# Which PSUM bank holds each head's exponents, and where the first four heads stand in TensorE's order

## The reference

```
x = x + gat(LN(x), adj)      # scores, softmax over allowed edges, probabilities @ wh
x = x + mamba2(LN(x))        # 8 heads, one chunk of 256 tokens
x = x + relational(LN(x))    # four relations, masks (adj == r) times x, times weight[r]
x = x + moe(LN(x))           # 8 experts, one per token, ReLU between two products
```

```
Lmat = exp(segsum(dA))
Y_diag = einsum('bcln,bcsn,bhcls,bcshp->bclhp', Cc, Bc, Lmat, xdt)
```

## Time and profile before

| | us |
|---|---|
| median of 3 runs | 3670.32 (3669.29 to 3671.39) |
| the profiled execution | 3668.25 |
| its span | 3666.5 |
| TensorE busy | 3470.5 (95%) |
| VectorE busy | 2562.8 (70%) |
| GpSimd busy | 1808.5 (49%) |
| ScalarE busy | 1776.8 (48%) |

### The profile page before, as it was taken

How to read it: one execution, slowest core, us unless ns; L and a number is a source line. 1 busy time by engine, 2 the same in 40 slices (tenths; PEclk the granted TensorE clock), 3 DMA queues, 4 the chain that set the end, 5 groups by cost and what they waited for, 6 DMA issues and landing times.

```text
span 3666.5 us, 64685 instructions
## 1 busy us (share of the span) xinstructions
PE 3470.5 (95%) x20028; PEld 2838.1 (77%) x20028; DVE 2562.8 (70%) x7429; ACT 1776.8 (48%) x3627; POOL 1808.5 (49%) x2010
## 2 busy tenths in 40 slices
PE   7999999999999999999999999999699999999998
PEld 5777777777777777777777777777488888888887
DVE  5878888887888888788888878888444444444444
ACT  4556655655655555565565556555232323323232
POOL 3545554454554545545454554545354555545453
PEclk8999999999999999999999999999799999999999
DMA  3121111111111111111111111111155555556563
GB/s 104 39 46 36 35 40 43 37 42 41 37 38 40 40 37 46 37 37 40 37 42 35 46 37 37 40 38 33 58 199 194 196 190 193 193 192 197 194 196 128
DMA packets 166001, 301.92 MB, mean 82 GB/s; under 512 B 37376, under 2 KB 138240, under 8 KB 147776
## 3 DMA queue, kind: packets, MB, share of 16 engines
q0 software_dynamic: 38272, 196.40, 15.7%
q1 hardware_dynamic: 91536, 70.58, 6.3%
q10 hardware_dynamic: 36144, 34.35, 6.0%
HBM read 248.61 MB, written 52.65 MB: 82 GB/s over the span
## 4 chain that ended last, share of the span: by engine, by line
PE 51%; DVE 26%; POOL 12%; issue 8%; ACT 1%; DVEq 0%; DMA 0%; ACTq 0%; POOLq 0%; SPq 0%
PE bank L1337 13%; PE bank L1351 13%; PE bank L1083 7%; POOL masks L466 7%; DVE conv L798 6%; PE bank L1101 5%; PE bank L1189 4%; DVE y L966 3%; PE bank L1289 3%; DVE y L971 2%; POOL row L452 2%; POOL rstd L452 2%; DVE stats L779 2%; DVE xn L789 1%; PE bank L1220 1%
## 5 line engine op out<-in xcount | busy, mean ns | idle before, releaser
L732 ACT ACTIVATE decay<-bank,w_up 128x256 f32<-128x256 f32 x568 | 269.4, 474 | 700.3 <-PE bank L1337 694.5
L1083 PE MATMUL bank<-xn1T,w_in 128*128 128x256 f32 x2304 | 523.4, 381 | 15.3 <-issue 14.3
L1337 PE MATMUL bank<-zs,w_up 128*128 128x256 f32 x2272 | 504.6, 380 | 0.6 <-ACT zs L590 0.6
L1351 PE MATMUL bank<-w_dn,decay 128*128 128x256 f32 x2272 | 502.1, 379 | 0.0
L1101 PE MATMUL bank<-w_rel,hT 128*128 128x256 f32 x2048 | 492.7, 384 | 0.0
L1083 PEld LDWEIGHTS bank<-xn1T,w_in 128*128 128x128 f32 x2304 | 434.1, 190 | 72.3 <-issue 14.0
L798 DVE SCALAR_TENSOR_TENSOR conv<-bank,conv_w,conv 128x255 f32<-128x255 f32 (+2 forms) x960 | 461.3, 481 | 34.8
L1337 PEld LDWEIGHTS bank<-zs,w_up 128*128 128x128 f32 x2272 | 433.4, 191 | 60.3 <-issue 0.9
L1351 PEld LDWEIGHTS bank<-w_dn,decay 128*128 128x128 f32 x2272 | 426.2, 190 | 55.1
L1044 DVE TENSOR_TENSOR hT<-bank,w_dn 128x256 f32<-128x256 f32 x142 | 60.3, 424 | 537.1 <-PE bank L1351 537.1
L1101 PEld LDWEIGHTS bank<-w_rel,hT 128*128 128x128 f32 x2048 | 368.9, 190 | 62.8 <-ACT hT L590 13.0
(11 more groups left out here) (219 smaller groups left out, 6341.4 us busy)
## 6 DMA issues: line engine op xcount, KB each, us to landing
token_rows<-row SPq DMA_DIRECT2D x64, 258.0 KB, 2.7
xT_sb<-in_xT ACTq DMA_DIRECT2D x64, 256.0 KB
x_sb<-in_x ACTq DMA_DIRECT2D x64, 256.0 KB, 2.7
adj_sb<-in_adj SPq DMA_DIRECT2D x64, 256.0 KB, 3.0
adjt_sb<-in_adjT SPq DMA_DIRECT2D x64, 256.0 KB, 3.0
out<-row SPq DMA_DIRECT2D x64, 256.0 KB, 2.2
w_in<-token_rows,idc POOLq DMA_INDIRECT x142
out<-hT,ids POOLq DMA_INDIRECT x142
```

The source lines that it names most:

```text
L732: nc.scalar.activation(hid(f), bank[f % 4][:, 0:GROUP], ACT.Relu, bias=b1[q % 2][:, f:f + 1]).then_inc(hid_ready, 1)
L1083: ins = mm(dst, w_in[:, k, first:first + P], xn1T[:, k, :], start=k == 0, stop=k == DK - 1)
L1337: ins = mm(bank[f % 4][:, 0:GROUP], w1[i][:, k, f * P:(f + 1) * P], xgT[:, k, :], start=k == 0, stop=k == DK - 1)
L1351: ins = mm(bank[4 + j][:, 0:D], hid(f)[:, j * P:(j + 1) * P], w2[i][:, f, :], start=f == 0, stop=f == FB - 1)
```

## The change

Each head gets a bank of its own choice, `EXPO = (2, 5, 1, 3, 4, 2, 5, 3)`. Head 2 uses bank 1, head 3 bank 3 and head 4 bank 4; heads 5, 6 and 7 take banks 2, 5 and 3 after the exponentials of heads 0, 1 and 3. Head 2 waits for `wh_ready`, head 3 for the first `xdt`, head 4 for the second. On TensorE `expo(range(0, 4))` moves in front of the turned probabilities. On ScalarE the exponentials of heads 0 and 1 move in front of the copy `probT`. The product of line 1249 waits in addition for the exponential of head 2.

```diff
-    EXPO = (2, 5, 3, 4)
+    EXPO = (2, 5, 1, 3, 4, 2, 5, 3)
 ...
                     ins.then_inc(prob_ready, 1)
-                    act.wait_ge(prob_turned, b1_ + 1)
-                    need(act, hp_made, b1_)
-                    copy(probT[:], bank[0][:, :]).then_inc(probT_ready, 1)
-                if b2_ is not None:
-                    for h in range(H):
+                for h in range(H):
+                    if h == 2 and b1_ is not None:
+                        act.wait_ge(prob_turned, b1_ + 1)
+                        need(act, hp_made, b1_)
+                        copy(probT[:], bank[0][:, :]).then_inc(probT_ready, 1)
+                    if b2_ is not None:
                         act.wait_ge(expo_made, 8 * b2_ + h + 1)
 ...
-                        nc.scalar.activation(decay[:, h, :], bank[EXPO[h % 4]][:, 0:TRI], ACT.Exp).then_inc(decay_ready, 1)
+                        nc.scalar.activation(decay[:, h, :], bank[EXPO[h]][:, 0:TRI], ACT.Exp).then_inc(decay_ready, 1)
 ...
-            def expo(heads, b):
+            def expo(heads, b, b1_):
 ...
-                    elif h in (2, 3):
-                        pe.wait_ge(xdt_ready, 2 * b + h - 1)
+                    elif h == 2:
+                        if b1_ is not None:
+                            pe.wait_ge(wh_ready, b1_ + 1)
+                    elif h in (3, 4):
+                        pe.wait_ge(xdt_ready, 2 * b + h - 2)
                     else:
-                        pe.wait_ge(decay_ready, 8 * b + h - 3)
+                        pe.wait_ge(decay_ready, 8 * b + {5: 1, 6: 2, 7: 4}[h])
 ...
                 if b3_ is not None:
                     relate(1, range(0, 2))
+                if b2_ is not None:
+                    expo(range(0, 4), b2_, b1_)
                 if b1_ is not None:
                     pe.wait_ge(prob_ready, b1_ + 1)
                     pe.wait_ge(wh_ready, b1_ + 1)
 ...
-                if b2_ is not None:
-                    expo(range(0, 4), b2_)
                 if b3_ is not None:
                     relate(1, range(2, R)).then_inc(gy_made, 1)
 ...
                     pe.wait_ge(probT_ready, b1_ + 1)
                     pe.wait_ge(wh_ready, b1_ + 1)
+                    if b2_ is not None:
+                        pe.wait_ge(decay_ready, 8 * b2_ + 3)
```

More of the change, by code:

```diff
@@ L1112, in expo @@
                         pe.wait_ge(g_ready, b + 1)
-                    elif h in (2, 3):
-                        pe.wait_ge(xdt_ready, 2 * b + h - 1)
-                    else:
-                        pe.wait_ge(decay_ready, 8 * b + h - 3)
-                    mm(bank[EXPO[h % 4]][:, :].rearrange("p (s l) -> p s l", s=T)[:, :, 0:P], identb[:],
+                    elif h == 2:
[3 more added lines that the diff above has]
+                        pe.wait_ge(xdt_ready, 2 * b + h - 2)
+                    else:
+                        pe.wait_ge(decay_ready, 8 * b + {5: 1, 6: 2, 7: 4}[h])
+                    mm(bank[EXPO[h]][:, :].rearrange("p (s l) -> p s l", s=T)[:, :, 0:P], identb[:],
                        negmask[:].unsqueeze(1).broadcast_to([P, T, P]), start=True, stop=True)
@@ L1121, in expo @@
                         q, u = h % 4, h // 4
-                        mm(bank[EXPO[q]][:, first:first + width], sel[32 * q:32 * q + 3 * H, u, :],
+                        mm(bank[EXPO[h]][:, first:first + width], sel[32 * q:32 * q + 3 * H, u, :],
                            cs3[32 * q:32 * q + 3 * H, l:N], start=False, stop=False, skip_group_check=True)
@@ L1126, in expo @@
                         q, u = h % 4, h // 4
-                        ins = mm(bank[EXPO[q]][:, first:first + width], cs3[32 * q:32 * q + 3 * H, s:s + P],
+                        ins = mm(bank[EXPO[h]][:, first:first + width], cs3[32 * q:32 * q + 3 * H, s:s + P],
                                  selneg[32 * q:32 * q + 3 * H, u, 0:width], start=False, stop=True,
@@ L1242, in step @@
                 if b2_ is not None:
-                    expo(range(4, H), b2_)
+                    expo(range(4, H), b2_, b1_)
                 if b1_ is not None:
```

## The result

| | median us | lowest to highest | runs |
|---|---|---|---|
| before | 3671.64 | 3669.29 to 3673.37 | 9 |
| changed | 3681.87 | 3680.31 to 3683.97 | 9 |

The ratio of changed to before is 1.0029, with a 95% interval of 1.0019 to 1.0039. Forecast were 3657 us and a range of 3642 to 3669; it came out slower, and past the range.

What follows compares the result with a forecast made beforehand. It took time to come only from TensorE's waits, with GpSimd's 0.18 us of slack before rsqrt(1) limiting plain steps. 29 x 0.4 = 11.6, with 1.2 at the start 12.8 us, gave 3657 us, range 3642 to 3669.

Steps and rivals of the forecast that it cites:

- What bounds the kernel: TensorE 95% busy; in plain steps two chains, VectorE's and GpSimd's masks, reach xn1 almost together, with 0.18 us GpSimd slack.
- Plain step, TensorE: In plain steps expo starts at 1052.52 without waiting for xdt; the rest of TensorE's work is 0.7 to 0.8 us early.
- ScalarE: In plain steps the exponentials come earlier, so VectorE's first two products can start at 1054.49 and 1055.73.
- Plain step, GpSimd: In plain steps the second mask meets no product and saves 0.75 us; rsqrt(1) comes 0.52 or 0.30 us sooner.
- The sum's term: Gain per plain step taken as 0.4 us, over 29 plain steps: 11.6 us.
- Routing step: In routing steps the second product meets the same mask hold and ends when it did: gain 0.
- Ends: In the third step the 2.54 us wait goes, expo is held by the first xdt: gain 1.2 us, bounds 0 and 2.5.
- E: Plain steps: first product gets in ahead of x2b's second instruction, GpSimd's chain grows 0.3 us; slower, 3678 us; 6%.
- F: A mask holds VectorE out for all its 1.5 us, second product 0.4 us later; slower, 3681 us; 4%.
- C: Collisions cost less than read, plain steps keep TensorE's full 0.8 us; 3646 us; 11%.
- D: TensorE merely waits later, GpSimd held as long as before, only 0.1 to 0.18 us left; 3665 us; 15%.
- B: Routing steps gain too, 31 x 0.4 = 12 us more; 3645 us; 14%.

Runs made afterwards that it cites:

- psum_after: Changed kernel with VectorE's products reading their second operand from PSUM bank 7 in place of g in SBUF; 3628.67 us, ratio 0.9888.
- after_x2b: Changed kernel with GpSimd's two x2b instructions moved in front of its wait for xdt; 3641.65 us, ratio 0.9923.
- h3plain: Changed kernel with VectorE's first product also waiting for head 3's exponential, in plain steps only; 3672.36 us, ratio 1.0007.
- expo_late: Changed kernel with TensorE's order alone undone: expo back behind the turned probabilities; 3684.67 us, ratio 1.0038.
- psum_before: Kernel before, with VectorE's products reading their second operand from PSUM bank 7 in place of g in SBUF; 3654.33 us, ratio 0.9958.

## Why the prediction was wrong

*What bounds the kernel* stood: GpSimd's 0.18 us of slack before `rsqrt(1)` in plain steps decided it, and the collisions were the right thing to look at.

*Plain step, TensorE* and *ScalarE* were right: `expo` at 1052.41 on the clock of before (forecast 1052.52), no wait for `xdt`, the products due at 1054.48 and 1055.77 (1054.49 and 1055.73).

*Plain step, GpSimd* is the step that failed. I let the second `x2b` hold the first product until 1054.5 or 1054.7, with a mask's hold of 0.4 us or half of it. It held until 1054.89, 0.58 us from its start: an instruction with two inputs of 256 columns, for which the trace of before had no row. The product's own hold then ended 0.2 to 0.4 us later than I had it, the first mask came up at 1055.87 and not at 1055.5 or 1055.7, and the second product, at 1055.77, was now ahead of it. I had it the other way round, the product held a little by the mask. The mask lost 0.71 us, and the delayed train met the fourth product with its third mask as well. The sum's term was 0.4 us gained a plain step and measured 0.53 lost. That the collisions make the loss is shown by psum_after, after_x2b and h3plain. That this one flip turned the sign is argued from the rows, since no run changes the length of `x2b`'s hold alone; the three odd steps of h3plain show what the order of such a pair can be worth.

The rule I read from before, who starts first keeps the other out, was right down to 0.04 us. I used it at a margin of 0.03 to 0.2 us with a hold that I had only bounded by a different instruction, and let the bounds of that hold move the gain between 0.30 and 0.52 without asking whether the order could flip. The rows of before already left it open: the 0.4 us is what the product lost, and counted from the mask's start the hold is 0.46 (1015.34 + 1.36 - 0.96 - 1015.28). With 0.46 the first mask comes at 1055.75, and the second product was due at 1055.73. A smaller slip has no effect on the term: by the rows GpSimd is free for `rsqrt(1)` at 1063.0 or 1063.2, not 1062.8 or 1063.0, and VectorE's input is due then too.

*Routing step*: gain 0 was right (41.35 against 41.34); `row` stands 5.89 us behind `xdt` in both. It was right with luck. The second product was forecast 0.08 us behind the second mask; it comes up within 0.02 us of it, and is held for 0.48 us all the same (0.95 us without a hold). The routing step of the changed kernel, VectorE and then GpSimd:

```profile
1018.45 1.44 DVE L807 TENSOR_TENSOR decay<-decay,g 128x768 f32<-128x768 f32 x1
...
1016.99 4.42 POOL L466 TENSOR_SCALAR masks<-adjt_sb 128x512 fp32r<-128x512 int32 x3
```

The three masks are whole, 4.42 us, and the second of them starts at 1018.47.

*Ends*: right. The first interval is 1.31 us shorter and the next two 0.16 each, where I had put 1.2, and `expo` is held by the first `xdt` as forecast.

*The rivals.* E had the right side, the right engine and a near time (3678), but another trigger: the product did not get in ahead of `x2b`. F is refuted: a mask never held a product for its full length; in after_x2b two run at 0.96 and 0.98 us within masks. C was half right: 0.7 to 0.9 us is there to be had in plain steps, once GpSimd does not collide. D, that TensorE merely waits later, is what h3plain shows, where a wait keeps the product late; the changed kernel was slower than that. B did not occur, but it hung on the 0.02 us of the routing step. The 10% given to slower was too little for a sum that hung on an order of starts 0.1 us apart.

## What to carry to other kernels

Before making one engine's work earlier, lay the other engine's train of instructions beside it and ask which pairs change places; where two starts are 0.1 us apart, both orders belong in the range, on both sides of zero. When a step ends on two chains with 0.2 us between them, shorten both: here neither the new order (10 us slower) nor the moved `x2b` (no difference) was worth anything alone, and together they gave 28 us. Work that waits for nothing in the contested stretch, as `x2b` did, is best put in front of it.

## What the runs showed of the hardware

- A VectorE product of 768 columns with two SBUF inputs keeps a GpSimd instruction out for about 0.8 us of its 0.96. A GpSimd instruction that is first keeps the product out only for its first part. For a mask of 1.5 us that is 0.46 to 0.48 us from its start, whether the product comes 0.06 us behind it (before), 0.21 (routing steps of the changed kernel) or 0.34 (plain steps of expo_late). For an addition of two inputs of 256 columns it is 0.58 of 0.73 us, read at one distance only (0.17 us behind its start). The Trainium skill ("SBUF — State Buffer", section "SBUF: two separate sides") gives the first instruction the ports for its whole length; for GpSimd that did not hold in any run here.
- Which of the two is first shows in the traces only down to a point. Where the recorded starts are 0.04 us apart or more, the first one keeps the other out, for as long as its hold lasts. At 0.02 us or less they do not tell: the same pair fell 21 times to the product and 3 times to the mask in h3plain.
- The smallest instruction loses as much time as a large one: one column took 0.91 us in place of 0.19.
- With the product's second operand in PSUM, products, masks and powers overlapped with no delay that shows: products 0.94 to 0.96 us, masks 1.47, the first power 0.72 (psum_after, psum_before).
